# A graph network on one core: attribute slots in pairs on one weight load, index tables by bitwise and, a third PSUM bank with block 2's product ahead in propagations 3 and 4, and block 12's check at another place

## What is computed

```python
# two SAGE convolutions, a residual and a layer norm
h = relu(mean_of_neighbours(x) @ W_l1.T + b_l1 + x @ W_r1.T)
y = layernorm(x + mean_of_neighbours(h) @ W_l2.T + b_l2 + h @ W_r2.T)
# three layers, batch norm and relu between them, then a residual and a layer norm
m   = concat([h[dst], h[src], edge_attr]) @ W.T + b      # self loops added, with attributes 1
agg = relu(segment_sum(m, dst))
```

## Time and profile before

| | us |
|---|---|
| median of 3 runs (lowest, highest) | 1181.01 (1178.44, 1189.15) |
| the profiled execution | 1185.87 |
| its span, first to last instruction | 1184.0 |
| build | 0 to 441 |
| propagation 0 | 441 to about 500 |
| propagations 1, 2, 3, 4 (with normalise before 3 and 4) | to 662, 808, 984, 1175 |

### The profile page before, as it was taken

One profiled execution on the slowest core, in us unless ns is written; L12 is line 12 of the kernel. 1 busy time (PEld: TensorE's weight loads), 2 busy tenths in 40 slices (PEclk: granted clock), 3 DMA queues, 4 the chain that ended last, 5 costly groups with the idle time before them and its releaser, 6 DMA issues. The chain is left out here.

```text
span 1184.0 us, 21105 instructions
## 1 busy us (share of the span) xinstructions
PE 1054.0 (89%) x8433; PEld 656.5 (55%) x8433; DVE 711.7 (60%) x1415; ACT 368.8 (31%) x733; POOL 104.9 (9%) x125
## 2 busy tenths in 40 slices
PE   0259999999999997999999999996899998899993
PEld 0258888899999984445555444443344444344441
DVE  5698979899899852623434755444555654233434
ACT  2475667686776530200000011113310105100000
POOL 4121212232211110000000000000000000000001
PEclk9968888899898897999999999998899998899997
DMA  6325535646455448963875436745036745037740
GB/s 160 48 69 196 187 112 204 201 135 234 126 173 170 120 171 254 404 257 127 311 277 219 164 118 267 290 150 218 14 122 240 289 179 218 18 122 270 287 181 22
DMA packets 67310, 216.89 MB, mean 183 GB/s; under 512 B 32176, under 2 KB 45227, under 8 KB 53667
## 3 DMA queue, kind: packets, MB, share of 16 engines
q1 hardware_dynamic: 59188, 164.51, 39.2%
q0 software_dynamic: 8016, 50.95, 12.0%
HBM read 170.68 MB, written 44.74 MB: 182 GB/s over the span
## 5 line engine op out<-in xcount | busy, mean ns | idle before, releaser
L1325 PE MATMUL PM<-Aring,Xop 128*128 128x512 fp8e4 (+1 forms) x1960 | 398.5, 363 | 0.0
L1325 PEld LDWEIGHTS PM<-Aring,Xop 128*128 128x128 f16 x1960 | 181.6, 98 | 216.6 <-issue 16.3
L1848 ACT ACTIVATE F<-PH,bag 64x512 f32<-64x512 f32 (+1 forms) x39 | 25.4, 657 | 382.4 <-PE PH L1544 382.3
L1325 PE MATMUL PM<-Ares,Xop 128*128 128x512 fp8e4 x588 | 137.0, 387 | 2.2 <-ACT Xop L1887 1.4
L772 PE MATMUL PW<-Aring 128*128 128x52 fp8e4 (+3 forms) x2151 | 115.9, 217 | 19.6 <-ACT F L836 17.6
L772 PEld LDWEIGHTS PW<-Aring 128*128 128x128 fp8e4 x2151 | 111.6, 103 | 22.8 <-ACT F L836 19.2
L785 PE MATMUL PA<-Ares,ea 128*128 128x32 f16 x1867 | 112.3, 235 | 0.0
L1681 DVE TENSOR_SCALAR S<-PM 128x256 f32<-128x256 f32 (+1 forms) x75 | 31.4, 418 | 130.6 <-PE PM L1325 118.8
L785 PEld LDWEIGHTS PA<-Ares,ea 128*128 128x128 f16 x1867 | 108.5, 116 | 0.0
L1325 PEld LDWEIGHTS PM<-Ares,Xop 128*128 128x128 f16 x588 | 55.9, 99 | 72.7 <-issue 10.0
L836 ACT ACTIVATE F<-PW 128x392 uint16<-128x392 f32 x196 | 85.4, 510 | 7.7 <-PE PW L772 5.4
(11 more groups left out here) (154 smaller groups left out, 1121.1 us busy)
## 6 DMA issues: line engine op xcount, KB each, us to landing
Aring<-adj SPq DMA_DIRECT2D x72, 1568.0 KB, 9.8
adj<-Aring POOLq DMA_DIRECT2D x12, 1568.0 KB, 6.1
adj<-Xop POOLq DMA_DIRECT2D x12, 1568.0 KB, 6.3
Ares<-adj SPq DMA_DIRECT2D x6, 1568.0 KB, 22.0
rc<-ea_sum SPq DMA_DIRECT2D x36, 128.0 KB, 5.8
eaf<-in_erow SPq DMA_DIRECT2D x62, 51.0 KB
Aring<-adj SPq DMA_DIRECT2D x4, 784.0 KB, 4.3
rc<-rc_d SPq DMA_DIRECT2D x12, 256.0 KB, 10.6
```

The costliest lines, as they stand in the source:

```text
L1325: last = nc.tensor.matmul(o, x[:, h, :], rhs, start=h == 0, stop=h == NT - 1)
L1848: nc.scalar.activation(F[0:64, c:c + w], PH[b % 2][0:64, 0:w], ACT.Relu, bias=t["bag"][:, 4 + conv:5 + conv]).then_inc(s_hr, 1)
```

## The change

- Attributes: two slots share one weight load. `eaf`'s high and low halves go to two groups of 32 columns each in a record of 80, a 65th column is one; `ohd` holds the one-hots of both slots side by side (64 columns), and PA has both sums interleaved. A slot of another window in the same pair takes a matmul of its own. `STEPS` has 1001 matmuls, 867 of two slots and 134 of one.
- The remainder is computed by VectorE in place in `eaf` (`s_rest`), and the low half is made of it by ScalarE in `low(c)`, which now gives `s_lo`. low stands behind table in ScalarE's list. `high` has one instruction instead of two.
- `sums` copies four pieces instead of one, and GpSimd adds the two halves before the DMA.
- Tables: B's one-hot and value come out of one bitwise and, D's out of scalar_tensor_tensor; digits has three short operations more; the evacuation's scale is a column instead of a number.
- Propagations: three banks PM (PC is gone), main(b) waits for sums(b - 3); in 3 and 4 main(2) comes at i = 1, ahead of post(0). block 12's check comes ahead of sums(11).

```diff
-                onehot(B[:], 8, 8, d[:, 1])
-                wait = tick(onehot(D[:, 0:w], w, 42, d[:, 3]))
+                onehot(B[:].bitcast(i16), 8, 8, d[:, 5], ALU.bitwise_and)
                 onehot(A[:], 8, 0, d[:, 0])
+                for i in range(w):
+                    nc.vector.scalar_tensor_tensor(Dv[:, t % 2, i, :], d[:, 3], 4.0 * i, d[:, 4], ALU.is_equal, ALU.mult)
...
-                v.wait_ge(s_own, wait)
-                valued(Bv[:], B[:], 8, d[:, 4])
-                valued(Dv[:, t % 2, 0:w], D[:, 0:w], w, d[:, 5]).then_inc(s_sm, 1)
...
                 v.wait_ge(s_hi, c + 1)
-                nc.vector.scalar_tensor_tensor(ea16[:, r, 0:n, 16:32], ea16[:, r, 0:n, 0:16], -LO, eax[:, c % 2, 0:n, :],
-                                               ALU.mult, ALU.add).then_inc(s_lo, 1)
+                x = eaf[:, c % 3, 0:n, 0:16].rearrange("p (g s) c -> p g s c", s=2)
+                nc.vector.tensor_tensor(x, x, part(r, n, 0), ALU.subtract).then_inc(s_rest, 1)
...
-                    for i in range(n):
-                        w, j = PSLOT[c * CH + i]
-                        st = w // 8
-                        if j == 0 and w % 8 == 0 and st >= 2:
+                    for w, j, e, f, start, stop in STEPS[c]:
+                        st, o = w // 8, w % 8 * 2 * PD
+                        if start and w % 8 == 0 and st >= 2:
                             pe.wait_ge(s_eas, st - 1)
-                        last = nc.tensor.matmul(PA[st % 2][:, w % 8 * PD:w % 8 * PD + PD],
-                                                ea_flat[:, c % 4, i * 33:i * 33 + 128], ohd[:, c % 4, :, i],
-                                                start=j == 0, stop=j == PJ[w] - 1)
+                        last = nc.tensor.matmul(
+                            PA[st % 2][:, o:o + 2 * PD].rearrange("p (d e) -> p d e", e=2)[:, :, e:f],
+                            ea_flat[:, c % 4, j * GW:j * GW + 128], ohd[:, c % 4, j, :, e:f], start=start, stop=stop)
...
-                nc.scalar.copy(ea16[:, r, 0:n, 0:16], eaf[:, c % 3, 0:n, 0:16])
-                nc.scalar.mul(eax[:, c % 2, 0:n, :], eaf[:, c % 3, 0:n, 0:16], LO).then_inc(s_hi, 1)
+                nc.scalar.copy(part(r, n, 0),
+                               eaf[:, c % 3, 0:n, 0:16].rearrange("p (g s) c -> p g s c", s=2)).then_inc(s_hi, 1)
+
+            def low(c):
+                n = min(CH, NPS - c * CH)
+                act.wait_ge(s_rest, c + 1)
+                nc.scalar.mul(part(c % 4, n, 16), eaf[:, c % 3, 0:n, 0:16].rearrange("p (g s) c -> p g s c", s=2),
+                              LO).then_inc(s_lo, 1)
...
-                nc.scalar.copy(eas[:, st % 2, 0:n], PA[st % 2][0:33, 0:n]).then_inc(s_eas, 1)
+                for e, to in enumerate([eas, odd]):
+                    of = PA[st % 2][:, 0:2 * n].rearrange("p (n e) -> p e n", e=2)[:, e]
+                    nc.scalar.copy(to[0:32, st % 2, 0:n], of[32 * e:32 * e + 32])
+                    last = nc.scalar.copy(to[32:33, st % 2, 0:n], of[64:65])
+                last.then_inc(s_eas, 1)
...
                 if h % 2 and h // 2 + 3 < TS:
                     table(h // 2 + 3)
+                for c in CHUNKS[h] if h < NH else []:
+                    low(c)
...
+                        nc.gpsimd.tensor_tensor(eas[:, st % 2, 0:n], eas[:, st % 2, 0:n], odd[:, st % 2, 0:n],
+                                                ALU.add).then_inc(s_add, 1)
...
-            if b >= 2:
-                pe.wait_ge(s_S, b - 1)
+            if b >= 3:
+                pe.wait_ge(s_S, b - 2)
...
-            if p >= 1 and (1 if p < 3 else 2) <= i < NB and not slow:
+            if p >= 3 and not slow and i == 1:
+                main(CAUGHT)
+            if p >= 1 and (1 if p < 3 else CAUGHT + 1) <= i < NB and not slow:
                 main(i)
...
+            if (p, i) == (2, NB - 1):
+                check(i)
             if 1 <= i <= NB:
                 sums(i - 1)
...
-        if p == 2:
-            check(NB - 1)
```

More of the change, by code:

```diff
@@ L169 @@
 CH = 32
+GW = 80
 NCH = -(-NPS // CH)
@@ L181, with steps @@
 LANDED = [sum(16 * len(PIECES[c]) for c in range(i % 3, i + 1, 3)) for i in range(NCH)]
+def steps():
+    found, seen = [], {w: set() for w in range(NPW)}
+    for c in range(NCH):
+        slots = PSLOT[c * CH:c * CH + CH]
+        whole = []
+        for i, (w, j) in enumerate(slots):
+            if whole and whole[-1][0] == w and i % 2:
+                whole[-1][3] += 1
+            else:
+                whole.append([w, i // 2, i % 2, i % 2 + 1, j])
+        for i in range(len(whole) - 1):
+            (w, _, e, f, j), (w2, _, e2, f2, _) = whole[i:i + 2]
+            if w == w2 and j == 0 and f - e < 2 and f2 - e2 == 2:
+                whole[i], whole[i + 1] = whole[i + 1], whole[i]
+        cuts = []
+        for w, g, e0, e1, _ in whole:
+            e = e0
+            while e < e1:
+                f = e + 1
+                while f < e1 and (f in seen[w]) == (e in seen[w]):
+                    f += 1
+                cuts.append([w, g, e, f, not seen[w], False])
+                seen[w] |= set(range(e, f))
+                e = f
+        found.append(cuts)
+    last = {cut[0]: cut for cuts in found for cut in cuts}
+    for cut in last.values():
+        cut[5] = True
+    return found
+STEPS = steps()
 CHUNKS = [range(max(0, h - 1) * NCH // (NH - 1), h * NCH // (NH - 1)) for h in range(NH)]
@@ L192 @@
 CHECKED = [(p, b) for p, blocks in ROUNDS for b in blocks]
+CAUGHT = 2
 EARLY = 3584
@@ L334, in build @@
         dig = within(0, [128, 8, 128], i16)
-        base = within(0, [128, 2, 128], i16)
+        base = within(0, [128, 1, 128], i16)
+        one = within(0, [128, 128], u16)
+        level = within(0, [128, 1], f32)
         warm = within(0, [128, TS], f32)
@@ L583, in digits, with onehot @@
                 op(d[:, 4], node, 4, 0x20, ALU.logical_shift_left, ALU.bitwise_and)
[L584 to L586 removed]
+                op(d[:, 5], src, 1, 7, ALU.logical_shift_right, ALU.bitwise_and)
+                op(d[:, 6], node, 6, 0x40, ALU.logical_shift_left, ALU.bitwise_and)
+                op(d[:, 7], src, 3, 8, ALU.logical_shift_left, ALU.bitwise_and).then_inc(s_dig, 1)
                 v.wait_ge(s_dig, 2 * t + 1)
[L588 to L592, removed]
+                tt, u = nc.vector.tensor_tensor, d.bitcast(u16)
+                wait = tick(tt(d[:, 4], d[:, 4], d[:, 6], ALU.bitwise_or))
+                over = tick(tt(d[:, 5], d[:, 5], d[:, 7], ALU.bitwise_or))
+                v.wait_ge(s_own, wait)
+                own(tt(d[:, 4], d[:, 4], base[:, 0], ALU.bitwise_or))
+                v.wait_ge(s_own, over)
+                tt(u[:, 5], one[:], u[:, 5], ALU.logical_shift_left)
+                tt(u[:, 4], u[:, 4], u[:, 1], ALU.logical_shift_left).then_inc(s_dig, 1)
+            def onehot(to, n, first_, table, how=ALU.is_equal):
                 shape = [128, n, 8, 16]
@@ L596, in onehot @@
                     io[:, first_:first_ + n, :].rearrange("p v (o s) -> p v o s", o=1).broadcast_to(shape),
[L597 to L601, removed]
+                    table.rearrange("p (o g s) -> p o g s", o=1, s=16).broadcast_to(shape), how)
             def small(t):
```

70 lines of the change are left out of this document (37 added, 33 removed).

## The result

| | before | after |
|---|---|---|
| median (lowest, highest) | 1182.45 us (1178.44, 1189.15), 4 runs | 1238.42 us (1236.54, 1239.39), 4 runs |
| ratio after / before | | 1.0465, 95% interval 1.0414 to 1.0517 |
| profiled span | 1184.0 us | 1232.8 us |

The change makes the kernel 56 us slower where the prediction had 1178 (1138 to 1203). Slower was the less likely side (0.28), and the time lies 35 us above the range.

The account below looks back on a forecast made before the run. VectorE and TensorE were both full; late buffer release would set the build's pairs. Build +12.6 and propagations -15.8 gave -3.2 on the profiled 1185.9 us, which lies 4.9 above the median, so 1178 us (1138 to 1203).

Parts of the forecast that it names:

- the loop: Build: low() frees an eaf buffer, its load follows, high() waits for it; late pairs 27.3 us instead of 24.5, +19.6.
- a load 4.7: Build, inside the loop: from an eaf buffer's release to the landing of its next load, 4.7 us.
- Rival 2: Build: 1.6 MB matrix writes hold loads, second landing up to 3.6 us later; +26, 1204 us; chance 0.18.
- rival 3: Build: GpSimd's 25 additions hold VectorE 0.4 us each; +10, 1188 us; chance 0.05.
- The loop is short there: Build before h = 6, where VectorE waits for TensorE's backlog: -3 us (bounds 0 and -7).
- The tail: Build's end behind VectorE's last large(): TensorE alone ends it, some 80 attribute matmuls go, -4 us (bounds -2 and -5).
- TensorE's saving: Build: 1867 attribute matmuls become 1001 at 60 ns each, so 52 us of TensorE go.
- 23.6 of VectorE's own work: Build: VectorE's work in one pair without a gap, a floor of 23.6 us under 24.5; 23.5 after the change.
- The propagations, -15.8: Behind the build: earlier product 2 in propagations 3 and 4 and block 12's earlier check together save 15.8 us.
- the check of block 12: Behind propagation 2: the check moves into VectorE's idle time, shortening ScalarE's wait before normalise, -4.1 us.
- propagation 4: Product 2 fills TensorE's idle time while factors arrive; without checks, 1034.5 instead of 1041.48, -7.0 us.
- propagation 3: Product 2 runs early, but post(1) waits for sums(1) behind VectorE's check; product 3 at 862.0 instead of 866.70, -4.7 us.

Follow-up runs that it names:

- run 9: The changed kernel with only the additions of the attribute halves moved from GpSimd to VectorE, low() still late: 1227.6 us, ratio 1.040 to before.
- run 10: The changed kernel with every write of the matrix issued twice, the second to a place nobody reads: 1305.1 us, ratio 1.103 to before.
- low_early: The changed kernel with low() moved from behind the table to right behind the evacuations in ScalarE's list: 1173.5 us, ratio 0.994 to before.
- run 6: low_early with the addition of the two attribute halves on VectorE instead of GpSimd: 1162.7 us, ratio 0.985 to before.
- run 11: low_early with the addition on VectorE and a fourth eaf buffer as well, tables included: 1157.6 us, ratio 0.978 to before.
- props_alone: The kernel before with the changes of the propagations alone (third PM bank, early product 2, block 12's early check): 1168.5 us, ratio 0.991.
- run 8: low_early without the change's tables and with the addition on VectorE: 1156.7 us, ratio 0.979 to before.

## Why the prediction was wrong

**The mechanism was right, the step that decides mis-sized.** The prediction named the loop, and where nothing disturbs it its pairs (25.5 us up to h = 14, 27.3 behind) nearly hold: those from h = 10 to 18 take 26.9, 26.9, 25.9 and 27.7 us, and the loads of that stretch 3.8 to 5.0 where 4.7 stood. What failed is the step "a load 4.7" for loads beside a write. From h = 18 to 28 the five pairs take 30.6, 32.5, 31.9, 31.9 and 30.2. The four long loads in them are together 13.0 us above 4.7 each (9.5, 8.0, 7.1, 7.2), the four between them 1.2; the additions are worth 5.3 (run 9). Together 19.5 us, against the 19.4 by which h = 14 to 28 exceeds the forecast (39.0 - 19.6). That it comes out so closely is in part luck: it takes each microsecond of a load as one of the pair, and in run 9 the same four loads are also 1.4 us shorter. These pairs are a third of the miss of the build; of the 55.8 us by which it exceeds the forecast (68.4 - 12.6), 23.3 lie before h = 14, 2.1 in the pair from h = 28 and 11.0 in the tail.

**Rivals that add up were weighed as alternatives.** Rival 2 (writes hold loads, 0.18) and rival 3 (additions hold VectorE, 0.05) both held, on top of the forecast's loop. Rival 2 has the right place, the buffers freed in odd h, and run 10 shows its price for a whole write, 4 us; rival 3 was priced at 0.4 us an addition where about 0.8 was measured. All three together, 1178 + 26 + 10 = 1214, would have lain above the range, and no case was made of it. The copies with a scale were counted as nothing; the tables as a whole cost 5.6 to 7.1 us, where the forecast had 0.

**The start and the first pairs.** "The loop is short there" was wrong: +8.8 instead of -3 and +12.5 instead of +1. With either cure of the loop they are 110 and 97 us, so they hang on it. The buffers of c = 8 and 12 (h = 5 and 7) became free at 102.5 and 137.6, beside writes issued at 103.00, 133.42 and 135.19, and their loads took 7.3 and 7.8 us, where I had 3.8 for few pieces: 7.4 us of it. The remainder of these 23 us was not broken down.

**The tail.** Predicted -4, measured +7.0. The reasoning that TensorE alone ends the build did not see that the last load of all (c = 58) stands in the same loop: freed at 473.3 beside a write at 473.13, 8.0 us. In run 9 it took 3.3, its three pieces issued before the write there or with it (467.12 to 468.15, the write at 468.11), and the tail 28.7 instead of 35.2. With the loop cured (low_early) the tail is still 36.1, with a last load of 9.7 us; run 6 has 31.9. What else sets it is open.

**TensorE's saving** came larger than counted, 66 us instead of 52 (a matmul of 29 ns at the full clock where 60 was taken), and was worth nothing while ScalarE could not follow. With the loop and the additions cured, 14 to 28 takes 170.7 (run 6) against 171.7 before, though TensorE is busy only 130.7 us of it. VectorE is busy 164.6 of it, 23.5 us a pair: the prediction's 23.6 of VectorE's own work was right as the next bound in the mean (single pairs take 21.5 to 25.8), but no run reached it; the best, run 11, has 24.1 a pair.

**The propagations, -15.8.** In sum they were close: -12.6 alone, -19.6 in after, of which 3.4 are the start of the layers (TensorE's first matmul behind its idle time there is at +22.9 us instead of +26.3). The parts, by the time between like instructions in before, in props_alone and in after: the check of block 12 -4.1 (TensorE's transposes behind normalise wait 4.02 us instead of 8.16), as predicted; propagation 4, up to its last product, -7.3 and -6.3 for -7.0; propagation 3 -1.9 and -3.9 for -4.7. What was missed in the last: TensorE runs dry before post(1), as foreseen, and its clock falls. props_alone in propagation 3, timeline and then busy time by stretch:

```profile
844.02 1.07 PE L1543 MATMUL PH<-S,ws 128*64 128x512 f32 x2
...
849.49 1.94 PE L1543 MATMUL PH<-S,ws 128*64 128x512 f32 x2 [3.54 <-DVE F L1691]
...
853.07 12.00 PE L1325 MATMUL PM<-Aring,Xop 128*128 128x512 fp8e4 x49
```

```profile
845.00:853.00 8.00, 4.46 (x7) 0.82 (x5) 6.71 (x11) 0.68 (x1) 0.00 (x0) 0.74 0.05 16
853.10:865.00 11.90, 11.90 (x50) 4.99 (x49) 8.38 (x9) 0.68 (x1) 0.00 (x0) 0.89 0.04 11
```

The four matmuls of post(1) take 3.6 us instead of 1.9, product 3 12.0 instead of 10.7, at a granted clock of 0.74 and 0.89, so partly at 1.2 GHz, after 3.54 us idle. So 3.0 us of the 4.7 went. Before, 5.90 us of idle time stood ahead of post(0) and cost such time there: its four matmuls took 3.6 us as well, and product 2 11.04. In after TensorE is idle 2.70 us before post(1), product 3 takes 11.05 us and propagation 3 gains 3.9; in run 8 it is idle 2.97, product 3 takes 10.75 and the gain is 4.2. So the longer of these two gaps cost no clock (granted 1.00 behind it) and the shorter one did (0.56 in post(1)); the length of the gap alone does not tell.

## What to carry to other kernels

When a step that frees a buffer is moved to another engine, follow the loop release, load, first use, and give it slack first: here an earlier place in the list or one buffer more was worth 65 or 63 us, more than the 56 that the change lost. Rivals that lengthen the same loop add up, so the range must hold their sum and not only each alone. And a helper engine's arithmetic is not free because the helper is idle: ask whose operands it shares.

## What the runs showed of the hardware that was not expected

- 25 GpSimd additions of 33x256 f32, 860 ns each in the mean, cost the kernel some 21 us while GpSimd did them (10.8 us more than with VectorE doing them, in two pairs of kernels, if VectorE's own 10.0 us all lie on the path); the same on VectorE takes 405 ns each.
- Weight load and matmul of 64 columns follow each other every 29 ns at the full clock and every 53 at half (46 in the mean, 1001 in 46.2 us); those of 32 columns before, with operands laid out otherwise, every 57 and 58 (60 in the mean).
- In after, loads whose buffer is freed within 2 us of a 1.6 MB write take 7.1 to 9.5 us from c = 14 on instead of 3.8 to 5.8, and 11.0 to 12.2 with two writes; one whose pieces were all issued before the write took 4.6.
- A copy out of PSUM of 128x392 elements takes 598 ns with a scale for each partition and 510 without.
